# Expert tiles of two 64-row blocks instead of four 32-row blocks, with half of the weights read in place

## The chip, the cores and the metric

One core of one Trainium2 chip. The metric is the device time in microseconds (us) of one execution, the median of several runs. The hardware profiler recorded one further execution; all durations come from it.

## The reference

A transformer block in fp32: layer norm and attention over 2 x 1024 tokens of 256 features, then a mixture of experts. Each of 2048 tokens goes to 4 of 60 experts (8192 choices) and through one shared expert. Cut to the part that the change touches:

```
logits = x @ gate_w.T                          # 2048 x 60
weights, sel = top_k(softmax(logits), 4)
for each expert e:                             # w13_e 352 x 256, w2_e 256 x 176
    gu = x @ w13_e.T
    h  = silu(gu[:, :176]) * gu[:, 176:]
    y += cw[:, e] * (h @ w2_e.T)
out = x + shared(x) + y
```

## The kernel before

The kernel runs attention first, then the shared expert (a hand-written order, `after`, of gate-up, down and routing steps), and last the expert loop over tiles.

**Tiles and blocks.** A tile is 128 rows, cut into `PER` = 4 blocks of `BLK` = 32 rows. A block holds choices of one expert only; an expert with n choices has ceil(n/32) blocks. How many blocks there are is known only on the device, so the loop has a fixed count that suffices for every routing: `NTILE` = ceil((8192/32 + 59)/4) = 79. The tiles that hold choices come first; the rest are padding, computed all the same and scattered to rows that nobody reads. `cnt_i[.., 3, e]` says how many tiles are needed up to expert e.

**Weights.** SP loads the experts in order into a ring of 8 slots (`load_expert`, `refill`): expert e goes out when the last tile of expert e - 8 is done (`tiles_done`). It announces expert e - 2 in `weights_arrived` after the load of e has gone out. A tile's word in `packed` holds the ring slot of each of its blocks and its last expert. VectorE copies each block's gate and up weights (704 elements on 128 partitions) from the ring to `placed13` (`place_gate_up`). ScalarE copies 3 of 4 blocks' down weights (all 4 in each fourth tile), and VectorE the rest, to `placed2`.

**One tile.** PE turns the rows (`turn_rows`, p_xs), multiplies by gate and up (`gate_up`, p_gu: for each of two halves of the features, a matmul for each block, on its own columns of the array), turns h (`turn_h`, p_hT) and multiplies by down (`down`, p_y). VectorE takes the turned rows out (`evacuate`, xsT) and multiplies (hh). ScalarE makes silu (hg), takes hT out (`turn`) and weighs the result into one of `NYS` = 8 buffers (`weigh`, ys). GpSimd scatters ys to `expert_out`; the buffer is free again when the scatter that used it 8 tiles before has landed. In PE's order, iteration i holds turn_rows(i+2), turn_h(i-2), gate_up(i) and down(i-3); the others keep the same order.

**Rows.** GpSimd gathers each tile's 128 rows with one indirect DMA into `xs_low` and `xs_top`, 48 places together. 48 gathers go out before the loop, most of them 4 after each gate-up of the shared expert; the other 31 take places that become free, and are spread over tiles 0 to 62.

**The end.** SP waits until the last tile that holds choices has been scattered, then loads the results in 24 pieces (`fin`). VectorE adds them up, in program order behind all `NTILE` tiles, and SP stores them.

Of the kernel before, what the change touches and what calls it, by code (L numbers as in the profile page):

```python
# [5 lines left out]
def attention_moe_block(nc, x_in, wq_in, wk_in, wv_in, wo_in, gate_in, w13_in, w2_in,  # L6
# [9 lines left out]
    P = 128  # L16
# [25 lines left out]
    PER = 4  # L42
# [11 lines left out]
    N13, N2 = 3, 4  # L54
# [27 lines left out]
    with ctx:  # L82
# [38 lines left out]
        gather_i = keep("gather_i", [P, NTILE], i32)  # L121
# [124 lines left out]
        NXS = min(NTILE, LOW // ROW) // LG * LG  # L246
        xs_low = moe("xs_low", [P, NXS, ROW])
        sb(sm, "low_rest", [P, LOW - used_moe[0]]) if LOW > used_moe[0] else None
        used_moe[0] = 0
        placed2 = moe("placed2", [P, N2, PER, 2 * C])  # L250
# [3 lines left out]

        moe("slot0_kept", [P, PROBS + SLOT_Q - used_moe[0]])
        placed13 = moe("placed13", [P, N13, PER, W13])
        picks = moe("picks", [P, 2, LG, TOPK])
        cw = moe("cw", [P, NTILE])
        ys = moe("ys", [P, NYS, C])
        xsT = moe("xsT", [P, 2, C])  # L260
        MID = PROBS + 3 * SLOT_Q + KV
# [3 lines left out]
        xsT2 = sb(sm, "xsT2", [P, C])  # L265

        NXT = 8
        xs_top = sb(sm, "xs_top", [P, NXT, ROW])
        sm.close()
        xsT = [xsT[:, 0, :], xsT[:, 1, :], xsT2[:, :]]  # L270
# [4 lines left out]
        LAST_TOP = FULL + 2 * LG  # L275
        AGAIN = LAST_TOP - NXS - NXT

        def xs_at(i):

            if i < NXS + NXT:  # L280
                return i, None
            if i < LAST_TOP:
                return i - NXS - NXT, i - NXS - NXT
            return NXS + i - LAST_TOP, NXS + i - LAST_TOP

        def xs_rows(i, n=1):
            at = xs_at(i)[0]
            return xs_low[:, at:at + n, :] if at < NXS else xs_top[:, at - NXS:at - NXS + n, :]

        assert NXS + NXT <= FULL and NTILE - LAST_TOP <= NXT and not (NXS % LG or NXT % LG or LAST_TOP % LG)  # L290

        PART = TQ * C
        LAST_SLOT = (E - 1) % RING
        assert (FULL - NXS - NXT) * ROW >= TOPK * PART and LOW - AGAIN * ROW >= TOPK * PART
        assert LAST_SLOT * WE >= 3 * PART + PART // 2 and (RING - 1 - LAST_SLOT) * WE >= TOPK * PART + PART // 2
        sf = ExitStack()
        fin2 = sb(sf, "fin2", [P, TOPK, TQ, C])
        sb(sf, "rows_kept", [P, AGAIN * ROW - TOPK * PART])  # L300
        fin1 = sb(sf, "fin1", [P, TOPK, TQ, C])
        sb(sf, "mid_kept", [P, LOW - AGAIN * ROW - TOPK * PART + MID])
        fin3 = sb(sf, "fin3", [P, TOPK - 1, TQ, C])
        fin3_a = sb(sf, "fin3_a", [P, 2, C])
        sb(sf, "last_expert_kept", [P, (LAST_SLOT + 1) * WE - 3 * PART - PART // 2])
        fin0 = sb(sf, "fin0", [P, TOPK, TQ, C])
        fin3_b = sb(sf, "fin3_b", [P, 2, C])
# [130 lines left out]
        w2_placed_low = sem("w2_placed_low")  # L438
        w2_placed_high = sem("w2_placed_high")
        xs_loaded = [sem(f"xs_loaded{q}") for q in range((NXS + NXT) // LG)]  # L440
# [97 lines left out]
        def results(k, from_, to):  # L538
            c = from_ // TQ
            from_, to = from_ - c * TQ, to - c * TQ  # L540
            if c == NCH - 1 and k == TOPK - 1:
                return fin3_a[:, from_:to, :] if to <= 2 else fin3_b[:, from_ - 2:to - 2, :]
            return (fin0, fin1, fin2, fin3)[c][:, k, from_:to, :]

        def group_loaded(q):

            n = min(LG, NTILE - q * LG)
            return xs_loaded[xs_at(q * LG)[0] // LG], 16 * (n if q * LG < NXS + NXT else LG + n)

        def downs_on_act(i):  # L550

            return PER if i % 4 == 3 else PER - 1

        def downs_on_dve(i):
            return sum(PER - downs_on_act(n) for n in range(i + 1))
# [125 lines left out]
        def _(pool):  # L681
# [193 lines left out]
            gathered = NXS + NXT - 4 * (NCH * NFS - THIRD)  # L875
            for i in range(gathered):
                gather(i)
            for n in range(THIRD, NCH * NFS):
                pool.wait_ge(sgu_in_psum, n + 1)
                for _ in range(4):  # L880
                    gather(gathered)
                    gathered += 1

# [9 lines left out]
            for n in range(rest):  # L893
                due.setdefault(max(n * (NTILE - 14) // rest, xs_at(gathered + n)[1] + 3), []).append(gathered + n)
# [8 lines left out]
        def _(act):  # L903
# [96 lines left out]
            def place_down(i, from_, to, tile=None):  # L1000
                if from_ == 0:
                    tile = act.value_load(packed[0:1, i:i + 1])
                    if i >= N2:
                        act.wait_ge(tiles_done, i - N2 + 1)
                    wait_apart(act, weights_arrived, tile >> (3 * PER))
                for h in range(from_, to):
                    last = copy(placed2[0:FH, i % N2, h, :], ring[0:FH, W13:][:, bass.ds(ring_at(tile, h), 2 * C)])
                if to == downs_on_act(i):
                    last.then_inc(w2_placed_low, 1)
                return tile  # L1010
# [17 lines left out]
            for i in range(NTILE + 3):  # L1028
                if 2 <= i < NTILE + 2:
                    turn(i - 2)  # L1030
                if i < NTILE:
                    tile = place_down(i, 0, 2)
# [4 lines left out]
                    place_down(i, 2, downs_on_act(i), tile)  # L1037
# [4 lines left out]
        def _(dve):  # L1042
# [368 lines left out]
            def blocks():  # L1411
# [16 lines left out]
                for h in range(PER):  # L1428
# [6 lines left out]
                count(v.scalar_tensor_tensor(out=two[:, 0:2], in0=slots[:, 1:4:2], scalar=float(RING),  # L1435
                                             in1=slots[:, 0:4:2], op0=ALU.mult, op1=ALU.add))
                count(v.scalar_tensor_tensor(out=four[:, 0:1], in0=two[:, 1:2], scalar=float(RING ** 2),
                                             in1=two[:, 0:1], op0=ALU.mult, op1=ALU.add))
                count(v.scalar_tensor_tensor(out=four[:, 1:2], in0=whose[:, 3:4], scalar=float(RING ** PER),
                                             in1=four[:, 0:1], op0=ALU.mult, op1=ALU.add))  # L1440
# [62 lines left out]
            def place_gate_up(i, from_, to, tile=None):  # L1503
                if from_ == 0:
                    tile = dve.value_load(packed[0:1, i:i + 1])
                    if i >= N13:
                        dve.wait_ge(gu_in_psum, i - N13 + 1)
                    wait_apart(dve, weights_arrived, tile >> (3 * PER))
                for h in range(from_, to):
                    last = v.tensor_copy(placed13[:, i % N13, h, :], ring[:, bass.ds(ring_at(tile, h), W13)])  # L1510
                if to == PER:
                    last.then_inc(w13_placed, 1)
                return tile

            def place_down(i, tile):
                if i >= N2:
                    dve.wait_ge(tiles_done, i - N2 + 1)
                for h in range(downs_on_act(i), PER):
                    v.tensor_copy(placed2[0:FH, i % N2, h, :], ring[0:FH, W13:][:, bass.ds(ring_at(tile, h), 2 * C)])\
                        .then_inc(w2_placed_high, 1)  # L1520
# [7 lines left out]
            words = {}  # L1528
            for kind, c, f in after:
# [24 lines left out]
                elif kind == "down" and (c < NCH - 1 or f):  # L1554
                    for q in (2 * f, 2 * f + 1):
                        add_shared(c, q)
                elif kind == "down":

                    h_low_part(NCH * NFS - 1)
                    words[0] = place_gate_up(0, 0, PER)  # L1560
                    add_shared(c, 0)
                    words[1] = place_gate_up(1, 0, PER)
                    add_shared(c, 1)
                elif kind not in ("soft", "late"):
                    on_bench(kind, c, f)
# [15 lines left out]
            for i in range(NTILE):  # L1581
# [5 lines left out]
                if i + 2 < NTILE:  # L1587
                    words[i + 2] = place_gate_up(i + 2, 0, PER - 1)
# [5 lines left out]
                if i + 2 < NTILE:  # L1594
                    place_gate_up(i + 2, PER - 1, PER, words[i + 2])
                place_down(i, words.pop(i))
# [13 lines left out]
        def _(pe):  # L1610
# [246 lines left out]

            def gate_up(i):
# [90 lines left out]
```

## Time and profile before

| what | value |
|---|---|
| median of 3 runs | 739.28 us (736.56 to 745.55) |
| span of the profiled execution | 799.1 us |
| TensorE clock granted, mean | 0.927 |
| busy: PE, DVE, ACT, POOL | 689.1, 482.4, 507.8, 379.1 us |
| attention, shared expert and routing | 0 to 517 us |
| expert loop | 517 to 776 us |
| adding up and storing | to 799 us |

The span reaches from the first to the last instruction. The profiled execution has no other time of its own on record, and its span is 59.8 us longer than the median of the runs. PE is TensorE (PEld its weight loads), DVE VectorE, ACT ScalarE, POOL GpSimd, SP the engine that issues most DMAs.

### The profile page before, as it was taken

The numbers are of one execution on the slowest core, as the hardware profiler recorded it, in microseconds if no ns is written. First come the engines' busy times: TensorE is split into PE (matmuls) and PEld (weight loads), VectorE is DVE, ScalarE is ACT, GpSimd is POOL, SyncE is SP. The second block draws the span as 40 slices with busy tenths as digits, with TensorE's granted clock in tenths as the row PEclk, the third lists the DMA queues.
The fourth block names the chain that finished last, engine by engine and source line by source line (L and its number), as shares of the span: only waits on it lengthen the run. The fifth ranks groups of instructions, "written<-read, shape, count | busy, mean of one in ns | idle before, by whom it ended". The sixth has DMA issues, their size and how long they took to land.

```text
span 799.1 us, 17758 instructions
## 1 busy us (share of the span) xinstructions
PE 689.1 (86%) x5591; PEld 349.4 (44%) x5591; DVE 482.4 (60%) x1335; ACT 507.8 (64%) x865; POOL 379.1 (47%) x376
## 2 busy tenths in 40 slices
PE   3788999999999999987979667699899988989970
PEld 2433333434333443366758455444344433434430
DVE  5784533564524545256864213399587957968957
ACT  2586888878689888922222102099587968868950
POOL 2173242234322293343034727158754875886850
PEclk9799999999899999999989878699889999998985
DMA  5000000000040000092011313146656666765188
GB/s 173 0 2 1 1 1 1 1 1 28 28 135 1 28 28 27 29 215 56 27 3 54 107 32 103 27 128 201 196 162 215 198 186 208 211 193 150 55 276 310
DMA packets 42941, 75.88 MB, mean 95 GB/s; under 512 B 7864, under 2 KB 23676, under 8 KB 42852
## 3 DMA queue, kind: packets, MB, share of 16 engines
q1 hardware_dynamic: 33476, 53.81, 22.1%
q0 software_dynamic: 9376, 20.97, 9.3%
q8 instruction: 45, 0.74, 0.4%
q14 instruction: 44, 0.36, 0.2%
HBM read 58.07 MB, written 16.67 MB: 94 GB/s over the span
## 4 chain that ended last, share of the span: by engine, by line
PE 65%; DVE 13%; issue 7%; another core or an unknown queue 5%; DMA 3%; SPq 3%; ACT 2%; POOL 1%; DVEq 1%; ACTq 0%; POOLq 0%
PE p_o L1694 15%; PE p_gu L1865 10%; PE p_s L1682 10%; PE p_y L1886 6%; PE p_xs L1855 3%; PE bench L1629 2%; SPq L670 2%; PE p_hT L1875 2%; PE p_d L1796 2%; PE bench L1616 1%; PE p_d L1797 1%; PE p_d L1798 1%; PE bench L1730 1%; PE bench L1708 1%
## 5 line engine op out<-in xcount | busy, mean ns | idle before, releaser
L969 ACT ACTIVATE probs<-p_s 128x1024 f32<-128x1024 f32 x256 | 243.8, 1039 | 52.1 <-PE p_s L1682 50.1
L886 POOL DMA_INDIRECT expert_out<-ys,goes_to x79 | 134.7, 1704 | 81.0 <-ACT ys L905 62.8
L905 ACT ACTIVATE placed<-ring 88x512 f32 x256 | 150.4, 626 | 31.3 <-PE p_d L1798 23.4
L1510 DVE COPY placed<-ring 128x704 f32 x316 | 151.7, 520 | 29.1 <-SPq L651 12.2
L1694 PE MATMUL p_o<-probs,vext 128*32 128x512 f32 x1024 | 138.2, 614 | 0.2 <-DVE enr L1176 0.2
L1865 PE MATMUL p_gu<-placed,xsT 128*32 128x352 f32 x1264 | 122.4, 473 | 5.7 <-issue 5.4
L866 POOL DMA_INDIRECT xs_low<-x_rows,choice_i x64 | 76.3, 1191 | 53.0 <-DVE choice_i L1479 17.5
L1682 PE MATMUL p_s<-qst,kst 64*128 64x512 f32 x512 | 95.8, 451 | 3.1 <-DVE kst L1359 1.6
L812 POOL DMA_INDIRECT members<-place,slot x48 | 47.8, 995 | 104.0 <-PE p_o L1694 85.6
L1886 PE MATMUL p_y<-placed,hT 88*32 88x256 f32 x1264 | 91.4, 392 | 2.2 <-ACT hT L905 1.2
L1682 PEld LDWEIGHTS p_s<-qst,kst 64*128 64x128 f32 x512 | 39.4, 185 | 82.3 <-ACT probs L969 62.7
L1886 PEld LDWEIGHTS p_y<-placed,hT 88*32 88x32 f32 x1264 | 45.4, 113 | 44.5 <-issue 30.3
L1865 PEld LDWEIGHTS p_gu<-placed,xsT 128*32 128x32 f32 x1264 | 35.5, 110 | 55.6 <-issue 53.4
L726 POOL TENSOR_TENSOR rc_t<-raw,cos 128x320 f32<-128x320 f32 (+2 forms) x16 | 11.3, 709 | 95.3 <-DVE qst L1369 61.9
L905 ACT ACTIVATE shT_h<-sh 128x512 fp32r<-128x512 f32 (+1 forms) x24 | 15.1, 631 | 64.5 <-PE p_d L1798 28.0
L1796 PE MATMUL p_d<-sdown_h,shT_h 128*128 128x256 f32 (+1 forms) x96 | 32.4, 338 | 18.7 <-DVE xres L1500 13.5
L905 ACT ACTIVATE ys<-p_y,cw 128x256 f32<-128x256 f32 x79 | 36.8, 466 | 15.9 <-remote 10.0
L989 ACT ACTIVATE sg<-p_g 128x512 f32<-128x512 f32 (+1 forms) x20 | 11.9, 594 | 46.9 <-PE p_u L1788 30.5
L1694 PEld LDWEIGHTS p_o<-probs,vext 128*32 128x32 f32 x1024 | 20.4, 108 | 39.5 <-issue 20.9
L1875 PE MATMUL p_hT<-ident,hh 128*88 128x128 f32 x158 | 31.2, 277 | 7.3 <-issue 4.9
L1036 ACT ACTIVATE hg<-p_gu 128x176 f32<-128x176 f32 x79 | 24.1, 305 | 20.2 <-remote 17.6
L1526 DVE COPY xsT<-p_xs 128x256 f32<-128x256 f32 x79 | 32.5, 412 | 5.4 <-remote 4.2
(262 smaller groups left out, 1117.7 us busy)
## 6 DMA issues: line engine op xcount, KB each, us to landing
ring<-in_w_dram SPq DMA_DIRECT2D x60, 352.0 KB
ring<-in_w_dram SPq DMA_DIRECT2D x60, 176.0 KB
fin<-expert_out SPq DMA_DIRECT2D x12, 512.0 KB, 8.6
x_rows<-rows SPq DMA_DIRECT2D x4, 520.0 KB, 3.6
x2T_kept<-xt SPq DMA_DIRECT2D x3, 512.0 KB, 3.6
x2r<-x2T_kept SPq DMA_DIRECT2D x3, 512.0 KB, 6.1
out_dram<-xres SPq DMA_DIRECT2D x3, 512.0 KB, 5.2
sup<-in_sup_dram SPq DMA_DIRECT2D x2, 704.0 KB
```

What stands on the lines that cost most here:

```text
L812: pool.indirect_dma_start(members, bass.IndirectOffsetOnAxis(ap=slot[:, n:n + 1], axis=0), place[:, n:n + 1], None).then_inc(scattered, 16)
L866: pool.indirect_dma_start(xs_rows(i)[:, 0, :], None, x2_rows, bass.IndirectOffsetOnAxis(ap=choice_i[:, 1, i:i + 1], axis=0))\
L886: pool.indirect_dma_start(expert_out, bass.IndirectOffsetOnAxis(ap=goes_to[:, i:i + 1], axis=0), ys[:, i % NYS, :], None).then_inc(y_out[i ...
L905: return nc.scalar.activation(o, i_, ACT.Copy, **kw)
L969: nc.scalar.activation(probs[:, j % NPB, :], p_s[j % NSB][:, :], ACT.Exp, scale=SCALE)\
L1510: last = v.tensor_copy(placed13[:, i % N13, h, :], ring[:, bass.ds(ring_at(tile, h), W13)])
L1682: last = mm(p_s[j % NSB][:, h * QC:(h + 1) * QC], kst[b][rows_, rr // 2, at], qst[rows_, c % 3, pair, :], start=True, stop=True)
L1694: last = mm(p_o[32 * g_:32 * g_ + 32, :], vext[c // 2][:, kb, rr // 2 + KP * h, :], probs[:, (2 * u + half) % NPB, h * QC:(h + 1) * QC], s ...
L1796: mm(p_d[q % 2][:, 0:C], h_high_, high, start=(f == 0), stop=False)
L1865: last = mm(p_gu[i % 2][h * BLK:(h + 1) * BLK, 0:F2], xsT[i % 3][:, k * P + h * BLK:k * P + (h + 1) * BLK], placed13[:, i % N13, h, k * F2 ...
L1875: last = tr(p_hT[i % 2][0:FH, k * P:(k + 1) * P], hh[:, i % 3, k * FH:(k + 1) * FH], ident[:, :])
L1886: last = mm(p_y[i % 2][h * BLK:(h + 1) * BLK, 0:C], hT[0:FH, i % 3, k * P + h * BLK:k * P + (h + 1) * BLK], placed2[0:FH, i % N2, h, k * C ...
```

## The change

Blocks have 64 rows and a tile has two of them, so a fixed count of 94 tiles. PE reads the first block's weights from the ring at an address from a register; only the second block's are copied: gate and up by VectorE, down by ScalarE. PE loads each tile's word for it. Every tile has its own place for its rows, so that no gather waits for a place; 26 gathers go out before the loop and 68 in it. `placed2` has 5 buffers instead of 4. The memory is laid out anew, and the results are loaded to one stretch.

```diff
-    PER = 4
+    PER = 2
     BLK = P // PER
     NTILE = -(-(TOK * TOPK // BLK + E - 1) // PER)
-    N13, N2 = 3, 4
+    N13, N2 = 3, 5
...
             def gather(i):
-                had = xs_at(i)[1]
-                if had is not None:
-                    pool.wait_ge(xsT_in_psum, had + 1)
-                    pool.wait_ge(picks_made, had // LG + 1)
-                elif i == NXS:
-                    pool.wait_ge(sgu_in_psum, (NCH - 1) * NFS)
+                if i == EARLY:
+                    pool.wait_ge(sdown_in_psum, NT)
...
-            gathered = NXS + NXT - 4 * (NCH * NFS - THIRD)
+            gathered = 4
...
-                for _ in range(4):
+                for _ in range(2):
...
-                due.setdefault(max(n * (NTILE - 14) // rest, xs_at(gathered + n)[1] + 3), []).append(gathered + n)
+                due.setdefault(n * (NTILE - 14) // rest, []).append(gathered + n)
...
+            def place_down(i):
+                tile = act.value_load(packed[0:1, i:i + 1])
+                if i >= N2:
+                    act.wait_ge(tiles_done, i - N2 + 1)
+                act.wait_ge(w13_placed, i + 1)
+                copy(placed2[0:FH, i % N2, :], ring[0:FH, W13:][:, bass.ds(ring_at(tile, 1), 2 * C)])\
+                    .then_inc(w2_placed, 1)
...
+            def place_gate_up(i):
+                tile = dve.value_load(packed[0:1, i:i + 1])
+                if i >= N13:
+                    dve.wait_ge(gu_in_psum, i - N13 + 1)
+                wait_apart(dve, weights_arrived, tile >> (3 * PER))
+                v.tensor_copy(placed13[:, i % N13, :], ring[:, bass.ds(ring_at(tile, 1), W13)]).then_inc(w13_placed, 1)
...
                 for k in range(KC):
                     for h in range(PER):
+                        weights = (placed13[:, i % N13, k * F2:(k + 1) * F2] if h else
+                                   ring[:, bass.ds(ring_at(words[i], 0) + k * F2, F2)])
                         last = mm(p_gu[i % 2][h * BLK:(h + 1) * BLK, 0:F2],
                                   xsT[i % 3][:, k * P + h * BLK:k * P + (h + 1) * BLK],
-                                  placed13[:, i % N13, h, k * F2:(k + 1) * F2], start=(k == 0), stop=(k == KC - 1))
+                                  weights, start=(k == 0), stop=(k == KC - 1))
...
+                if i + 1 < NTILE:
+                    words[i + 1] = pe.value_load(packed[0:1, i + 1:i + 2])
```

`down` changes as `gate_up` does. ScalarE's `place_down(i)` stands after its silu of tile i, VectorE's `place_gate_up` two tiles ahead, and PE's load of the next word between `gate_up(i)` and `down(i - 3)`.

## Rows read from the trace of the kernel before

**Rows 1.** The page's groups: line, engine, tiles, count | busy us, mean ns | idle.
```profile
L1510 DVE COPY placed<-ring 128x704 f32 x316 | 151.7, 520 | 29.1 <-SPq L651 12.2
L905 ACT ACTIVATE placed<-ring 88x512 f32 x256 | 150.4, 626 | 31.3 <-PE p_d L1798 23.4
L1865 PE MATMUL p_gu<-placed,xsT 128*32 128x352 f32 x1264 | 122.4, 473 | 5.7 <-issue 5.4
L1886 PE MATMUL p_y<-placed,hT 88*32 88x256 f32 x1264 | 91.4, 392 | 2.2 <-ACT hT L905 1.2
```

**Rows 2.** The timeline of PE in the expert loop: start us, length us.
```profile
545.19 1.39 PE L1865 MATMUL p_gu<-placed,xsT 128*32 128x352 f32 x16
546.40 1.05 PE L1886 MATMUL p_y<-placed,hT 88*32 88x256 f32 x16
547.38 0.44 PE L1855 MATMUL p_xs<-ident,xs_low 128*128 128x128 f32 x2
547.66 0.38 PE L1875 MATMUL p_hT<-ident,hh 128*88 128x128 f32 x2
547.97 1.39 PE L1865 MATMUL p_gu<-placed,xsT 128*32 128x352 f32 x16
...
564.61 1.39 PE L1865 MATMUL p_gu<-placed,xsT 128*32 128x352 f32 x16
```

**Rows 3.** The same timeline for VectorE.
```profile
547.09 1.38 DVE L1510 COPY placed<-ring 128x704 f32 x3
...
548.40 0.33 DVE L1592 TENSOR_TENSOR hh<-hg,p_gu 128x176 f32<-128x176 f32 x1
```

**Rows 4.** The timeline of PE at the loop's first tile and at tile 70.
```profile
517.33 1.39 PE L1865 MATMUL p_gu<-placed,xsT 128*32 128x352 f32 x16
...
743.83 1.39 PE L1865 MATMUL p_gu<-placed,xsT 128*32 128x352 f32 x16
```

**Rows 5.** The timeline of SP and VectorE at the end.
```profile
763.04 19.51 SPq L670 DMA_DIRECT2D fin<-expert_out  x15
...
770.25 0.42 DVE L1519 COPY placed<-ring 88x512 f32 x1
773.68 1.23 DVE L1602 TENSOR_TENSOR fin<-fin 128x1024 f32<-128x1024 f32 x1 [3.01 <-issue]
...
796.50 0.43 DVE L1607 TENSOR_TENSOR xres<-xres,fin 128x256 f32<-128x256 f32 x1
```

**Rows 6.** The stretch after the loop: busy us (x) of each engine.
```profile
771.00:799.00 28.00, 3.64 (x32) 1.61 (x32) 20.07 (x24) 1.69 (x5) 4.38 (x4) 0.51 0.95 329
```

**Rows 7.** GpSimd's groups, first in the loop, then ahead of it (425 to 505).
```profile
L886 POOL DMA_INDIRECT expert_out<-ys,goes_to x71 | 126.1, 1777 | 74.0 <-ACT ys L905 57.0 <-issue 14.9 <-PE p_xs L1855 1.9
L866 POOL DMA_INDIRECT xs_low<-x_rows,choice_i x24 | 37.6, 1567 | 7.3 <-issue 6.1 <-PE p_gu L1865 0.6 <-remote 0.6
L866 POOL DMA_INDIRECT xs_low<-x_rows,choice_i x40: 940/946/1166, 425.5 to 491.4; - x40
```

**Rows 8.** The timeline of GpSimd from its first scatter.
```profile
526.77 1.71 POOL L886 DMA_INDIRECT expert_out<-ys,goes_to  x1 [23.93 <-ACT ys L905]
...
560.07 1.44 POOL L866 DMA_INDIRECT xs_low<-x_rows,choice_i  x1 [0.30 <-issue]
```

**Rows 9.** The timeline of PE in two stretches where it slows down.
```profile
451.26 0.37 PE L1796 MATMUL p_d<-sdown_h,shT_h 128*128 128x256 f32 x1 [0.36 <-issue]
...
574.24 5.07 PE L1865 MATMUL p_gu<-placed,xsT 128*32 128x352 f32 x13 [0.30 <-issue]
```

**Rows 10.** Stretches before the loop: PE, PEld, DVE, ACT, POOL busy (x), clock, DMA.
```profile
448.00:468.00 20.00, 6.31 (x23) 3.86 (x22) 1.81 (x4) 0.60 (x1) 11.35 (x12) 0.65 0.33 87
495.00:507.00 12.00, 1.44 (x4) 1.07 (x5) 1.60 (x4) 0.00 (x0) 6.01 (x7) 0.50 0.30 79
```

**Rows 11.** Loads of the tile's word: ns min/median/max.
```profile
L1505 DVEq TENSOR_LOAD <-packed x79: 300/304/616, 492.9 to 761.7; - x79
L1002 ACTq TENSOR_LOAD <-packed x79: 273/278/787, 515.5 to 767.0; - x79
```

More of the change, by code:

```diff
@@ L264, in attention_moe_block @@
         ring = sb(sm, "ring", [P, RING * WE])
-        xsT2 = sb(sm, "xsT2", [P, C])
-        NXT = 8
-        xs_top = sb(sm, "xs_top", [P, NXT, ROW])
+        NTHIRD = NTILE - NFIRST - NSECOND
+        xs_third = sb(sm, "xs_third", [P, NTHIRD, ROW])
         sm.close()
-        xsT = [xsT[:, 0, :], xsT[:, 1, :], xsT2[:, :]]
+        xsT = [xsT[:, n, :] for n in range(3)]
         FULL = REAL // P
[L275 to L284, printed above, removed]
-        def xs_rows(i, n=1):
[L287 to L297, printed above, removed]
-        sf = ExitStack()
[L299 to L307, printed above, removed]
+        def xs_rows(i, n=1):
+            if i < NFIRST:
+                return xs_first[:, i:i + n, :]
+            if i < NFIRST + NSECOND:
+                return xs_second[:, i - NFIRST:i - NFIRST + n, :]
+            return xs_third[:, i - NFIRST - NSECOND:i - NFIRST - NSECOND + n, :]
+        assert NCH * TOPK * TQ * C <= FULL * ROW and FULL <= NFIRST
+        sf = ExitStack()
+        fin = [sb(sf, f"fin{c}", [P, TOPK, TQ, C]) for c in range(NCH)]
         sf.close()
@@ L539, in results @@
             c = from_ // TQ
[L540 to L543, printed above, removed]
+            return fin[c][:, k, from_ - c * TQ:to - c * TQ, :]
         def group_loaded(q):
             n = min(LG, NTILE - q * LG)
[L548 to L555, printed above, removed]
+            return xs_loaded[q % (NGRP // 2)], 16 * (n if q < NGRP // 2 else LG + n)
         def ring_at(tile, h):
@@ L998, in _ @@
             h_high_part(NCH * NFS - 1)
[L1000 to L1010, printed above, removed]
+            def place_down(i):
[5 more added lines that the diff above has]
+                    .then_inc(w2_placed, 1)
             def turn(i):
@@ L1434, in blocks @@
                 count(v.tensor_copy(slots, slot_i[:, :]))
[L1435 to L1437 removed]
+                count(v.scalar_tensor_tensor(out=two[:, 0:1], in0=slots[:, 1:2], scalar=float(RING),
+                                             in1=slots[:, 0:1], op0=ALU.mult, op1=ALU.add))
+                count(v.scalar_tensor_tensor(out=four[:, 1:2], in0=whose[:, 1:2], scalar=float(RING ** PER),
                                              in1=two[:, 0:1], op0=ALU.mult, op1=ALU.add))
[L1439 to L1440 removed]
                 v.tensor_scalar(eid_b[:, :], four[:, 1:2].to_broadcast([P, P]), float(RING ** PER), None, ALU.add)\
@@ L1883, in down @@
                     pe.wait_ge(y_ready, i - 1)
+                tile = words.pop(i)
                 for k in range(2):
                     for h in range(PER):
+                        weights = (placed2[0:FH, i % N2, k * C:(k + 1) * C] if h else
+                                   ring[0:FH, W13:][:, bass.ds(ring_at(tile, 0) + k * C, C)])
                         last = mm(p_y[i % 2][h * BLK:(h + 1) * BLK, 0:C],
                                   hT[0:FH, i % 3, k * P + h * BLK:k * P + (h + 1) * BLK],
-                                  placed2[0:FH, i % N2, h, k * C:(k + 1) * C], start=(k == 0), stop=(k == 1))
+                                  weights, start=(k == 0), stop=(k == 1))
                 last.then_inc(tiles_done, 1)
+            words[0] = pe.value_load(packed[0:1, 0:1])
             turn_rows(0)
```

72 lines of the change are left out of this document (25 added, 47 removed).

## The prediction

> **What bounds the kernel now.** I read the page's groups first, then the timeline of each engine inside the expert loop, then the end of the kernel.
>
> The groups show where the weights' copies lie: VectorE makes 316 copies of 520 ns for gate and up, ScalarE 256 copies of 626 ns for down, and PE spends 122.4 and 91.4 us on the two products [rows 1]. That looks like a loop that its copies hold up. The timeline says otherwise. Where the loop runs smoothly, PE's groups follow one another without a break: gate-up at 545.19, down at 546.40, turned rows at 547.38, turned h at 547.66, the next gate-up at 547.97 [rows 2]. Seven tiles take 564.61 - 545.19 = 19.42 us, so a tile takes 2.77 us, and all of it is PE's. VectorE is nearly as full but not the last: its copies start 0.43 us apart (three in 1.38 us, with ends that overlap) [rows 3], so 4.25 of them hold it for 1.83 us, and the rest of its tile (hh, xsT, picks) for some 0.7 us.
>
> The loop as a whole is slower. From the first gate-up to that of tile 70 it is 743.83 - 517.33 = 226.5 us [rows 4]. At 2.77 us 70 tiles are 194.2; the first three are 2.6 us shorter together, since no down product stands in them yet; so 34.9 us are excess. The reader is to see two candidates for it. PE itself slows down in places: 13 matmuls that wait for nothing spread over 5.07 us [rows 9]. And GpSimd's DMAs take 1.8 us (scatters) and 1.6 us (gathers) in the loop, but 0.97 us ahead of it [rows 7].
>
> The end has a limit of its own. SP starts to load the results at 763.04, 19.2 us after the gate-up of tile 70; VectorE has finished the padding tiles at 770.67 and waits for the loads until 773.68 [rows 4, 5]. It then adds for 20.07 us with waits between [rows 6], and the last store lands at 799.1.
>
> **How many tiles.** Counted from the reference's own inputs, the 60 experts get 84 to 200 choices. In blocks of 32 these are 284 blocks, 71 tiles; in blocks of 64 they are 154, 77 tiles. The trace agrees with the first: the loads of results begin behind tile 70. The fixed counts are 79 and 94, so padding grows from 8 tiles to 17.
>
> **Part 1, PE's time for a tile.** A matmul still streams 352 or 256 columns over the same two halves; half as many blocks stand side by side, each twice as wide. Now 16 matmuls of 473 ns fill only 1.21 us, so four run at once [rows 1, 2]. Two at once with half the count fill the same 1.21 us. I take 2.77 us again. Below: nothing becomes shorter, since no stream does. Above: if two wide blocks did not overlap, gate-up and down would take 2.2 us more; the overlap of four in the rows speaks against that. The Trainium skill, "TensorEngine Tiling (Array Packing)", Available Configurations and Theoretical Speedup, gives four tiles at 128x32 and two at 128x64, so the gain is 4x for 32 columns and 2x for 64. By that a 64-row block costs twice a 32-row block, as I have it, and the change earns PE nothing: it pays for more rows.
>
> **Part 2, registers on PE.** Each tile adds one load of the word and four addresses. Such a load takes 0.30 us on VectorE and 0.27 on ScalarE [rows 11]. The word of tile i + 1 is loaded behind gate_up(i), whose 1.2 us of matmuls run meanwhile; in front of it is nothing that waits, behind it are down(i - 3), and through it ScalarE's weighing and SP's refills. Between 0 and 0.30 us a tile, 0 to 28 us; I take 0, since the cover is four times as long. It would go if PE had to finish its queue before such a load.
>
> **Part 3, VectorE and ScalarE.** VectorE loses 3 of 4 copies and the quarter one (1.83 us to 0.43 a tile), ScalarE 1.75 of 2.75. Neither is the last engine, so by itself this is worth nothing. VectorE's word load stays. ScalarE's copy now waits for `w13_placed` behind the silu of the same tile; VectorE made that two tiles before, so the wait costs nothing, and behind it stand only weigh and turn. The ring: an expert takes 1.28 tiles instead of 1.18, so 8 slots last longer, and SP's refills come sooner than needed.
>
> **Part 4, GpSimd.** This is where the copies count. In the smooth stretch 13 DMAs go out between 526.77 and 560.07, one in 2.56 us [rows 8], against 0.97 + 0.30 us ahead of the loop [rows 7]. A tile needs one scatter and 31/65 of a gather, 1.48 DMAs or 3.8 us: more than 2.77. GpSimd falls behind by 1 us a tile until the 8 buffers ys are full, after some 15 tiles; then ScalarE's weighing waits for it. What it gets is the time between VectorE's copies: 2.77 - 1.83 = 0.94 us a tile for 1.08 DMAs, 0.87 us each. 1.48 DMAs need 1.29 us, so the pace is 1.83 + 1.29 = 3.12 us while gathers last, 50 tiles: 50 x 0.35 = 17 us. The Trainium skill, "SBUF — State Buffer", SBUF: two separate sides, names the cause: a DMA from GpSimd's queue needs descriptors written through ports that an fp32 SBUF-to-SBUF copy of VectorE holds. By that rule the rows' 0.97 against 1.6 to 1.8 us is no load of the DMA engines, and the change removes it.
>
> After the change a tile needs 1 + 68/80 = 1.85 DMAs: 1.85 x 1.27 = 2.35 us, plus one copy of 0.43, 2.78. That is on a par with PE and no more; a little above it costs nothing until 8 buffers are used up.
>
> How much of the 34.9 us does a timed run have? From above: 17 us, the sum just made. From below: the profiled span is 59.8 us longer than the median. In 448 to 468 and 495 to 507 PE is busy for 6.3 of 20 and 1.4 of 12 us while its matmuls wait for nothing, with the clock at 0.65 and 0.50 of full [rows 9, 10], so 24 us, and some 5 at half clock behind them, look like the recording's own. That leaves 31 of the 59.8 for the loop's 34.9, and 4 us in timed runs. I take the middle, 11 us, and let all of it go.
>
> **Part 5, the end.** Padding now ends last. After tile 76, 17 more tiles run in 47 us; the loads of results take some 24 of them. VectorE adds only behind tile 93: its hh ends 548.73 - 545.19 = 3.54 us after that tile's gate-up starts [rows 2, 3], the sums take 20.07 us without waits, and 2.2 us remain to the last store: 25.8 us after the gate-up of tile 93. Before, the end came 799.1 - 743.83 = 55.3 us after that of tile 70. A price from rows; between them lies 4 us if the loads still hold up the first sum.
>
> **Ahead of the loop.** 22 gathers fewer there, two reads of the blocks' members fewer: GpSimd only, nobody waits for them. Nothing.
>
> **The sum**, made against the profiled execution: 23 tiles more between the two gate-ups, 23 x 2.77 = +63.8; the end 25.8 - 55.3 = -29.5; together +34.3; less the 11 us of lag: +23.3. The difference is carried over to the median of the runs: 739.3 + 23.3 = 762.6, so 763 us, 3.2% slower.
>
> **The rivals.**
> - *The excess is real.* All or most of the 34.9 us is in timed runs, because of GpSimd, and goes. Then +34.3 - 34.9: 739 to 750 us, no change. For: 3.12 us a tile nearly explains it. Against: the 59.8 us. 0.27.
> - *Faster: the slow stretches of PE are real too, and come from bursts of gathers.* 48 gathers ahead of the loop fall to 26, and 24 us go as well: 739.3 - 0.6 - 24 = 715 us. It decides if these stretches are missing in the profile after. Against: they are just what the timed runs lack. 0.07.
> - *No lag at all in timed runs.* PE sets 2.77 us in both: 774 us. 0.25.
> - *The registers stop PE*, at its upper bound: 763 + 28 = 791 us. 0.10.
> - *The change does not do what it says*: if the last engine were VectorE or ScalarE, a tile would become shorter. Rows 2 leave no room for it.
>
> **How the numbers follow.** My forecast has 0.31, the rivals the rest. About 2% either way (724.5 to 754.1 us) is what a measurement of this kernel can tell from no change. Faster: 0.07. Within: 0.27. Slower: 0.31 + 0.25 + 0.10 = 0.66. The range from 738 to 786 us takes in the first and third rival, and leaves out the faster one and most of the last.
>
> **What would show it.** In the profile after: p_gu x752 with gate-up again 2.77 us apart (above that, parts 1 or 2 are wrong); placed copies x94 on each engine; GpSimd's DMAs near 1.1 us in the loop; loads of results 17 tiles before the loop's end, and VectorE's first sum straight behind its last hh. I would be wrong if timed runs before had the whole excess, or if PE's period changed.

## The result, and the profile after

| | before | after |
|---|---|---|
| median | 742.04 us (736.56 to 745.55, 4 runs) | 758.75 us (756.74 to 762.03, 4 runs) |
| ratio after/before | | 1.022, 95% interval 1.016 to 1.029 |
| profiled execution | span 799.1 us | span 756.8 us, own time 758.59 us |

The change made the kernel 16.7 us slower, 2.2%: clear of no change, though the interval does not tell whether it is more or less than 2%. But the two profiles can't simply be subtracted: the one of before was 60 us longer than its timed runs, and I had put part of this down to the recording. The experiments show what it was. They ran on four chips (all kernels of one section below on the same one). On the first the kernel before takes 741.5 us, on the other three 803.0, 802.4 and 798.5. The comparison above is from a chip of the first kind; the profile of before shows the times of the second. I call them quick and slow chips. Each of the four ran the experiments of one section only, at one time, so what differs may belong to the time and not to the chip; no run here separates the two. The partner for the profile after is therefore the second profile of before, from a quick chip (the first experiment).

The profile after, groups: line, engine, tiles, count | busy us, mean ns | idle.
```profile
L850 POOL DMA_INDIRECT expert_out<-ys,goes_to x94 | 96.6, 1028 | 79.4 <-ACT ys L869 74.4 <-issue 5.0
...
L1807 PE MATMUL p_gu<-ring,xsT 128*64 x376 | 131.4, 472 | 0.0
L1807 PE MATMUL p_gu<-placed,xsT 128*64 128x352 f32 x376 | 131.4, 472 | 0.0
...
L1465 DVE COPY placed<-ring 128x704 f32 x94 | 49.7, 529 | 39.3 <-SPq L618 21.3
...
L869 ACT ACTIVATE placed<-ring 88x512 f32 x94 | 59.4, 631 | 28.3 <-issue 26.0
```
Against [rows 1] a matmul is as long as before (472 and 473 ns), there are 752 instead of 1264, and only two stand side by side. So a tile's gate-up still takes 1.40 us (131.4 / 94; the two groups run over the same time), and there are more tiles. Against [rows 7] a scatter takes 1028 ns instead of 1777, and GpSimd now waits for ys (74.4 us): it is ahead of its work.

The same profile, PE's timeline at the gate-ups of tiles 0 and 93:
```profile
476.52 0.51 PE L1807 MATMUL p_gu<-ring,xsT 128*64 x1
...
732.33 0.51 PE L1807 MATMUL p_gu<-ring,xsT 128*64 x1
```
The same profile, busy time between these two: us, PE, PEld, DVE, ACT, POOL busy (x), clock, DMA.
```profile
476.52:732.33 255.81, 255.81 (x1832) 133.11 (x1831) 122.36 (x325) 144.41 (x366) 156.47 (x157) 1.00 0.74 225
```
PE is busy for all of the 255.81 us at a granted clock of 1.00: nothing holds it up in the loop, and VectorE and ScalarE are busy for about half of the time.

The same profile, SP and VectorE at the end:
```profile
700.13 24.58 SPq L637 DMA_DIRECT2D fin<-expert_out  x24
...
734.13 0.34 DVE L1533 TENSOR_TENSOR hh<-hg,p_gu 128x176 f32<-128x176 f32 x1 [2.21 <-ACT hg L995]
734.38 1.22 DVE L1540 TENSOR_TENSOR fin<-fin 128x1024 f32<-128x1024 f32 x1
```
The loads of results are all out at 724.7, and the first sum comes straight behind the last hh. Where [rows 5] have VectorE waiting for loads, the padding tiles now set the end.

### The profile page after: what moved, and what is told of

Read it like the earlier page. It is cut to its first block, busy times and chain, and to the rows that moved or that the text cites. A ratio compares the mean times of both kernels' runs of the same rounds, so it can differ in the third digit from the quotient of the medians.

```text
span 756.8 us, 15005 instructions
## 1 busy us (share of the span) xinstructions
PE 697.6 (92%) x4627; PEld 365.0 (48%) x4627; DVE 392.5 (52%) x1082; ACT 447.8 (59%) x748; POOL 333.4 (44%) x404
## 4 chain that ended last, share of the span: by engine, by line
PE 84%; DVE 13%; ACT 1%; issue 1%; DMA 1%; DVEq 0%; ACTq 0%
PE p_gu L1807 17%; PE p_o L1632 16%; PE p_s L1620 10%; PE p_y L1830 10%; PE p_xs L1793 5%; PE p_hT L1817 3%; PE bench L1567 2%; PE p_d L1734 2%; PE bench L1554 2%; PE p_d L1736 1%; PE p_d L1735 1%; PE bench L1668 1%; PE bench L1646 1%; PE bench L1684 1%; PE p_g L1724 1%; PE p_g L1725 1%
## 5 line engine op out<-in xcount | busy, mean ns | idle before, releaser
L850 POOL DMA_INDIRECT expert_out<-ys,goes_to x94 | 96.6, 1028 | 79.4 <-ACT ys L869 74.4
L1807 PE MATMUL p_gu<-ring,xsT 128*64 x376 | 131.4, 472 | 0.0
L1807 PE MATMUL p_gu<-placed,xsT 128*64 128x352 f32 x376 | 131.4, 472 | 0.0
L829 POOL DMA_INDIRECT xs_first<-x_rows,choice_i x80 | 77.9, 974 | 69.1 <-issue 19.8
L1830 PE MATMUL p_y<-ring,hT 88*64 x376 | 96.6, 379 | 0.0
L1830 PE MATMUL p_y<-placed,hT 88*64 88x256 f32 x376 | 96.6, 379 | 0.0
L869 ACT ACTIVATE placed<-ring 88x512 f32 x94 | 59.4, 631 | 28.3 <-issue 26.0
L1830 PEld LDWEIGHTS p_y<-ring,hT 88*64 88x64 f32 x376 | 51.1, 136 | 42.2 <-issue 28.1
L1465 DVE COPY placed<-ring 128x704 f32 x94 | 49.7, 529 | 39.3 <-SPq L618 21.3
L1807 PEld LDWEIGHTS p_gu<-ring,xsT 128*64 128x64 f32 x376 | 43.7, 136 | 46.0 <-issue 46.0
L1830 PEld LDWEIGHTS p_y<-placed,hT 88*64 88x64 f32 x376 | 51.0, 136 | 0.0
```

Source lines behind the costliest of these rows:

```text
L829: pool.indirect_dma_start(xs_rows(i)[:, 0, :], None, x2_rows, bass.IndirectOffsetOnAxis(ap=choice_i[:, 1, i:i + 1], axis=0))\
L850: pool.indirect_dma_start(expert_out, bass.IndirectOffsetOnAxis(ap=goes_to[:, i:i + 1], axis=0), ys[:, i % NYS, :], None).then_inc(y_out[i ...
L869: return nc.scalar.activation(o, i_, ACT.Copy, **kw)
L1465: v.tensor_copy(placed13[:, i % N13, :], ring[:, bass.ds(ring_at(tile, 1), W13)]).then_inc(w13_placed, 1)
L1807: last = mm(p_gu[i % 2][h * BLK:(h + 1) * BLK, 0:F2], xsT[i % 3][:, k * P + h * BLK:k * P + (h + 1) * BLK], weights, start=(k == 0), stop= ...
L1830: last = mm(p_y[i % 2][h * BLK:(h + 1) * BLK, 0:C], hT[0:FH, i % 3, k * P + h * BLK:k * P + (h + 1) * BLK], weights, start=(k == 0), stop= ...
```

## Experiments on a quick chip (before: 741.5 us)

All four kernels ran beside 13 runs of the kernel before (737.21 to 748.02 us).

**The kernel before again.** 

> The kernel before once more (with one bound more on the word that VectorE and ScalarE load), to get a second profile of it. My theory: the stretches in which PE slowed down belonged to that one execution; here they are missing, the span is near 740 us, and from the first gate-up to that of tile 70 it takes 196 to 209 us (191.6 at 2.77 us a tile, and 4 to 17 us of lag that GpSimd's DMAs cause). Rival: the excess of 35 us is real; then it takes 226 us again. Rival: no lag, 192 us.

Its edit, on both word loads, also in all kernels below (in those made from the kernel after, on VectorE's alone):
```diff
-                tile = dve.value_load(packed[0:1, i:i + 1])
+                tile = dve.value_load(packed[0:1, i:i + 1], min_val=..., max_val=...)
```
Measured: 740.08 us (737.85 to 746.8), ratio 1.001 (0.997 to 1.005), span of the profile 736.9. PE's timeline at the gate-ups of tiles 0 and 70:
```profile
478.24 1.39 PE L1865 MATMUL p_gu<-placed,xsT 128*32 128x352 f32 x16
...
674.50 1.39 PE L1865 MATMUL p_gu<-placed,xsT 128*32 128x352 f32 x16
```
The loop begins 39 us earlier than in [rows 4], and its 70 tiles take 196.26 us instead of 226.5. So the stalls of [rows 9, 10] are missing, and of the excess of 34.9 us only 4.7 are left. GpSimd lags all the same. The group of scatters in this profile:
```profile
L886 POOL DMA_INDIRECT expert_out<-ys,goes_to x79 | 128.1, 1622 | 24.1 <-issue 20.4 <-ACT ys L905 2.4 <-PE p_xs L1855 0.9
```
The timelines of ScalarE (tile 70's ys), GpSimd (its scatter) and SP:
```profile
690.40 0.50 ACT L905 ACTIVATE ys<-p_y,cw 128x256 f32<-128x256 f32 x1
...
698.68 1.14 POOL L886 DMA_INDIRECT expert_out<-ys,goes_to  x1 [0.30 <-ACT ys L905]
...
702.03 18.20 SPq L670 DMA_DIRECT2D fin<-expert_out  x15
```
The scatter of tile 70 starts 8.3 us behind its ys (3.6 us in the first profile, where stalls of PE had let GpSimd catch up). And the ys itself comes late, 15.9 us after the gate-up for 10.8 in the first profile, since ScalarE had to wait for a buffer:
```profile
679.81 0.47 ACT L905 ACTIVATE ys<-p_y,cw 128x256 f32<-128x256 f32 x1 [3.92 <-DMA expert_out<-ys,goes_to]
```
So the lag comes due at the end: the loads of results can't start before 702.03, and the end is 736.9 - 674.5 = 62.4 us behind tile 70's gate-up (55.3 in the first profile). This gives the account of the change on a quick chip, from span to span:

| | before | after | difference | forecast |
|---|---|---|---|---|
| first gate-up | 478.24 | 476.52 | -1.7 | 0 |
| to that of the last tile that sets the end (70, 93) | 196.26 | 255.81 | +59.6 | +63.8 - 11 |
| from there to the end | 62.4 | 24.5 | -37.9 | -29.5 |
| sum | 736.9 | 756.8 | +19.9 | +23.3 |

**No registers on PE.** 

> The kernel after, with PE reading both blocks' weights from the copies of the second block at constant addresses; PE loads no words. Left out: the first block's own weights. My theory: the word load and the addresses lie beside matmuls and cost nothing, so the time is that of the kernel after, 757 to 761 us. Rival: they stop PE by up to 0.30 us a tile; then the 94 tiles become up to 28 us shorter, 731 us, and the gate-ups stand closer than 2.79 us.


```diff
-                        weights = (placed13[:, i % N13, k * F2:(k + 1) * F2] if h else
-                                   ring[:, bass.ds(ring_at(words[i], 0) + k * F2, F2)])
+                        weights = placed13[:, i % N13, k * F2:(k + 1) * F2]
...
-                if i + 1 < NTILE:
-                    words[i + 1] = pe.value_load(packed[0:1, i + 1:i + 2])
```
(`down` likewise.) Measured: 759.25 us (758.73 to 765.0), ratio 1.024 (1.016 to 1.032). PE's timeline:
```profile
562.92 1.40 PE L1805 MATMUL p_gu<-placed,xsT 128*64 128x352 f32 x8
...
565.71 1.40 PE L1805 MATMUL p_gu<-placed,xsT 128*64 128x352 f32 x8
...
568.49 1.40 PE L1805 MATMUL p_gu<-placed,xsT 128*64 128x352 f32 x8
```
2.79 us a tile with and without registers, and from the gate-up of tile 0 to that of tile 93 it is 255.78 us for 255.81: word loads and addresses are free here. The rival falls.

**No padding tiles.** 

> The kernel after with 77 tiles, those that hold choices for these inputs, and no padding tile. My theory: the 17 padding tiles (47 us) then go, but the loads of results, which they covered, end last: the end comes some 55 us after the gate-up of tile 76 as it did after that of tile 70 before, so 685.4 + 55 = 741 us of span, 16 us less than the kernel after. Rival: the loads end earlier than that and all 47 us go, 712 us. Rival: the end does not depend on the padding, no change.


```diff
-    NTILE = -(-(TOK * TOPK // BLK + E - 1) // PER)
+    NTILE = 77
...
-        NTHIRD = NTILE - NFIRST - NSECOND
+        NTHIRD = LG
```
(The second edit keeps the room for the last tiles' rows as large as one group.) Measured: 730.33 us (728.68 to 732.78), ratio 0.986 (0.978 to 0.994), 28 us less than the kernel after. Tile 76's gate-up on PE, SP, and VectorE's first sum:
```profile
684.13 0.51 PE L1807 MATMUL p_gu<-ring,xsT 128*64 x1
...
694.00 21.49 SPq L637 DMA_DIRECT2D fin<-expert_out  x24
...
702.51 1.23 DVE L1540 TENSOR_TENSOR fin<-fin 128x1024 f32<-128x1024 f32 x1 [16.25 <-DMA fin<-expert_out]
```
Tile 76's gate-up in the kernel after:
```profile
685.44 0.51 PE L1807 MATMUL p_gu<-ring,xsT 128*64 x1
```
As I thought, the loads then end last, but they cost less: 727.7 - 684.1 = 43.6 us behind tile 76, not 55. The 55.3 us of before held 8 padding tiles and GpSimd's lag. Tile 76's down product no longer stands behind three padding tiles, so the loads start 9.9 us after its gate-up (14.7 in the kernel after). The 17 padding tiles take 732.33 - 685.44 = 46.9 us, and the end behind the last gate-up is 43.6 - 24.5 = 19.1 us shorter with them, so they cost 28 us, more than the whole change loses. This kernel holds for these inputs only, not for every routing.

**Busy VectorE, with waits.** 

> The kernel after with four more fp32 copies of 512 elements on VectorE in each tile (some 1.3 us), to a buffer that nobody reads. My theory: these copies block GpSimd's DMAs, as the copies of the kernel before did: a scatter and a gather take 1.6 to 1.8 us instead of 0.97 to 1.2; 1.85 of them a tile no longer fit into 2.79 us, ScalarE's weighing waits for buffers, and the time grows by 15 to 50 us although VectorE itself has room. Rival: the DMAs of before were slow for the weights' and rows' traffic; then they stay at 1.0 to 1.2 us and the time stays at 759 us.


```diff
+                if i >= 2:
+                    for n in range(4):
+                        if i > 2 or n:
+                            dve.wait_ge(junk_made, 4 * (i - 2) + n)
+                        v.tensor_copy(junk[:, :], xres[:, 2 * n:2 * n + 2, :].rearrange("p t c -> p (t c)"))\
+                            .then_inc(junk_made, 1)
```
Measured: 801.84 us (798.69 to 804.45), ratio 1.081 (1.072 to 1.090). The size is about as expected, the cause is not. VectorE's timeline:
```profile
599.71 0.53 DVE L1467 COPY placed<-ring 128x704 f32 x1 [0.20 <-issue]
600.16 1.80 DVE L1472 COPY junk<-xres 128x512 f32<-128x512 f32 x4
601.88 0.33 DVE L1541 TENSOR_TENSOR hh<-hg,p_gu 128x176 f32<-128x176 f32 x1
602.12 0.42 DVE L1479 COPY xsT<-p_xs 128x256 f32<-128x256 f32 x1
602.89 0.53 DVE L1467 COPY placed<-ring 128x704 f32 x1 [0.35 <-issue]
```
The group of scatters:
```profile
L852 POOL DMA_INDIRECT expert_out<-ys,goes_to x94 | 105.6, 1123 | 106.0 <-ACT ys L871 103.0
```
VectorE's own round is now 602.89 - 599.71 = 3.18 us, above PE's 2.79, and in it VectorE waits for no other engine; GpSimd still waits for ys. This run says nothing for the blocking of DMAs; these copies, with a wait before each, lengthen a scatter from 1028 ns to 1123.

## Experiments on a slow chip (before: 803.0 us)

**VectorE's copies alone.** 

> The kernel before, with VectorE's copies of gate and up cut to 8 of 704 elements behind the third tile; all else stays, the gathers and their places too. Left out: most of the gate and up weights that PE should read. My theory: VectorE's long copies are what makes GpSimd's DMAs slow in the loop; without them scatters and gathers take 1.0 to 1.1 us, scatters follow ys by 0.3 us instead of up to 20, and the time falls by some 10 to 12 us (4.7 us in the loop and some 7 us by which the loads of results start earlier), to 728 to 731 us. Rival: something else slows them (ScalarE's copies, the load of the queues, the places of rows that must come free); then the scatters still lag by some 15 us and the time stays within 3 us of 740.


```diff
+                wide = W13 if i < N13 else 8
-                    last = v.tensor_copy(placed13[:, i % N13, h, :], ring[:, bass.ds(ring_at(tile, h), W13)])
+                    last = v.tensor_copy(placed13[:, i % N13, h, 0:wide], ring[:, bass.ds(ring_at(tile, h), wide)])
```
Measured: 791.66 us (790.92 to 794.51) beside 803.0, ratio 0.986 (0.980 to 0.992): -11.3 us, the 10 to 12 that I had expected, though beside another time. GpSimd's group, here and in the first profile of before:
```profile
L886 POOL DMA_INDIRECT expert_out<-ys,goes_to x79 | 77.4, 980 | 150.6 <-ACT ys L905 143.9 <-issue 6.7
...
L886 POOL DMA_INDIRECT expert_out<-ys,goes_to x79 | 134.7, 1704 | 81.0 <-ACT ys L905 62.8 <-issue 16.1 <-PE p_xs L1855 1.9
```
With the long copies gone, and nothing else changed, a scatter falls from 1704 ns to 980, and GpSimd no longer lags. This is the shown part of the theory: in this kernel GpSimd's DMAs are slow only with VectorE's long copies. The Trainium skill, "SBUF — State Buffer", SBUF: two separate sides, says that such a copy keeps GpSimd from writing the descriptors of its DMAs. The trace agrees as to the effect; it shows nothing of the descriptors.

**Part of the copies back.** 

> The kernel after with 77 tiles and, on VectorE, three more copies of 704 elements a tile that follow one another without a wait between them, as in the kernel before (their source is the copy of the tile before, nobody reads them). The run with four copies of 512 elements had a wait before each and was slower because VectorE itself became the last engine, while GpSimd's DMAs stayed at 1.0 to 1.1 us. By my theory, that copies in one piece block GpSimd, the DMAs take 1.6 us or more, scatters fall behind, and the time is 10 to 40 us above that of 77 tiles without them (730 us). Rival: the port is no matter; the DMAs stay at 1.0 to 1.1 us, and with 2.4 us of VectorE's work in 2.79 the time stays within 3 us of 730.


```diff
+                if i > 2:
+                    dve.wait_ge(junk_made, i - 2)
+                if i >= 2:
+                    for n in range(3):
+                        last = v.tensor_copy(junk[:, n, :], placed13[:, (i - 1) % N13, :])
+                    last.then_inc(junk_made, 1)
```
(704 columns each, on top of the kernel with 77 tiles.) Measured: 753.05 us (750.08 to 755.37), ratio to this chip's before 0.938 (0.932 to 0.945). Its partner (730 us) ran on a quick chip, so the time decides nothing. GpSimd's group:
```profile
L852 POOL DMA_INDIRECT expert_out<-ys,goes_to x77 | 90.3, 1173 | 68.5 <-ACT ys L871 56.0 <-issue 12.6
```
Four copies in a row give 1173 ns, not the 1600 that I expected; the kernel before has 1704 with 4.25. So without the long copies the slowness goes, but adding copies does not bring it back. What else takes part in the kernel before was not tried: there ScalarE copies 3.25 blocks a tile and here 1, and the added copies read another buffer. The ratio of 0.938 was the first sign of something else: its first gate-up comes at 475.7 us, where the kernel before, on such a chip, has 517.33 [rows 4].

**The first block from the ring.** 

> The kernel before, four blocks of 32 rows, with PE reading each tile's first block of weights from the ring; VectorE copies 3 blocks of gate and up instead of 4, ScalarE 2 or 3 of down. My theory: VectorE has 0.45 us a tile more in which GpSimd's DMAs run free; the lag falls and most of the 12 us that it costs come back: 728 to 735 us, faster than both kernels. Rival: the lag does not come from VectorE's copies: 740 us.


```diff
+                        weights = (placed13[:, i % N13, h, k * F2:(k + 1) * F2] if h else
+                                   ring[:, bass.ds(ring_at(words[i], 0) + k * F2, F2)])
```
(`down` likewise.) VectorE now makes 3 copies of gate and up a tile and 0.5 of down (4 and 0.25 before), ScalarE 2.5 of down (3.25 before). Measured: 789.72 us (787.93 to 794.3), ratio 0.986 (0.979 to 0.993). The 728 to 735 us were for a quick chip; the gain of 13 us is about the one expected.
```profile
L886 POOL DMA_INDIRECT expert_out<-ys,goes_to x79 | 87.4, 1106 | 132.1 <-ACT ys L905 123.6 <-issue 7.8 <-DVE picks L1573 0.7
```
So one block fewer takes most of the slowness away: 1106 ns with VectorE's 3.5 copies a tile, 1704 with 4.25, 980 with almost none. ScalarE's copies are fewer here too, so the step from 4.25 to 3.5 is not VectorE's alone.

**No padding before.** 

> The kernel before with 71 tiles, no padding tile. My theory: padding costs the kernel before next to nothing, since its 8 tiles end at 703 us while the results' loads start at 702 us and their first lands at 712; what goes is the wait of tile 70's down product for three further tiles, as far as GpSimd's lag does not take its place: 732 to 740 us. Rival: all 8 tiles count, 22 us less, 718 us.


```diff
+    NTILE = 71
```
Measured: 787.22 us (785.36 to 789.8), ratio 0.982 (0.976 to 0.989): -15.8 us, twice what I allowed. From tile 70's gate-up to the end it is 783.6 - 738.1 = 45.5 us instead of 55.3; the tiles up to it are 4.9 us shorter, one execution against another. Padding was not free before either. This splits the loss on a quick chip, as an estimate across two kinds of chip: 28 - 16 = 12 us for more padding, 6 x 2.79 = 17 us for six more tiles that hold choices, less the 12 us that GpSimd's lag had cost (below).

## Experiments on a second slow chip (before: 802.4 us)

**The kernel after, here.** 

> The kernel after once more (with one bound more on the word that VectorE loads). The kernel before has run at 742 us on two occasions and at 803 us on a third, where, as in the first profile of it, PE stalls ahead of the loop. My theory: such stalls are a chip's answer to GpSimd's gathers in bursts, and the kernel after does not make these bursts; so it takes some 759 to 780 us whatever the kernel before takes beside it, and where that takes 803 it is faster by 3 to 5%. Rival: the stalls belong to the chip and hit both kernels; then the ratio stays 1.02 and it takes 815 to 820 us beside 803.

Measured: 792.39 us (789.56 to 797.08, 9 runs), ratio 0.990 (0.987 to 0.994). Here the change is no loss but a gain of 10 us, 1%. I had expected 759 to 780 us, and by the rival 815 to 820: both were wrong. The span is 789.7, PE's timeline at the gate-ups of tiles 0 and 93:
```profile
477.28 0.51 PE L1807 MATMUL p_gu<-ring,xsT 128*64 x1
...
765.23 0.51 PE L1807 MATMUL p_gu<-ring,xsT 128*64 x1
```
The busy time between them:
```profile
477.28:765.23 287.95, 271.25 (x1831) 134.79 (x1830) 116.25 (x325) 139.25 (x366) 156.77 (x157) 0.98 0.65 200
```
Against the first profile of before the loop starts 40.0 us earlier, takes 287.95 - 226.5 = 61.5 us more and the end 24.5 - 55.3 = 30.8 less: -9.4. The loop is 32 us longer than the same loop on the quick chip (255.81). The view of waits, 478 to 765 us, names what the engines waited for (us in total, times, longest):
```profile
ACT hg L995 <- remote: 32.9, 13, 3.9
...
DVE xsT L1471 <- remote: 29.2, 14, 4.7
...
ACT hT L869 <- remote: 16.8, 7, 3.7
...
ACT ys L869 <- remote: 14.0, 8, 2.3
```
"remote" is the profile's name for a wait that no instruction of this core ended. The profile after from the quick chip has no such line.

**Bursts of gathers in the kernel after.** 

> The kernel after with 40 gathers ahead of the loop instead of 26, four behind each gate-up of the shared expert as in the kernel before, and 54 in the loop instead of 68. My theory: where the kernel before takes 803 us, PE stalls ahead of the loop as it does in that kernel, the first gate-up comes at 505 to 517 us instead of 476, and the time grows by 25 to 40 us; where it takes 742 us nothing happens, within 3 us of the kernel after. Rival: bursts are no matter, no change in either case.


```diff
-                for _ in range(2):
+                for _ in range(4 if gathered < EARLY else 0):
```
Measured: 788.63 us (785.4 to 795.55), ratio 0.988 (0.979 to 0.997), so 4 us less than the kernel after (their runs overlap) and not 25 to 40 more. Yet the first half of the theory holds. Its timeline in the shared expert, where the gathers begin to come in a row:
```profile
441.44 0.28 PE L1734 MATMUL p_d<-sdown_h,shT_h 128*128 128x256 f32 x1
...
441.73 0.94 POOL L829 DMA_INDIRECT xs_first<-x_rows,choice_i  x1 [0.30 <-issue]
442.61 0.28 PE L1735 MATMUL p_d<-sdown_l,shT_h 128*128 128x256 f32 x1 [0.89 <-issue]
442.97 0.94 POOL L829 DMA_INDIRECT xs_first<-x_rows,choice_i  x1 [0.30 <-issue]
...
443.33 0.37 PE L1736 MATMUL p_d<-sdown_h,shT_l 128*128 128x256 f32 x1 [0.44 <-issue]
443.35 0.60 ACT L953 ACTIVATE sg<-p_g 128x512 f32<-128x512 f32 x1 [3.69 <-remote]
```
Matmuls that ran 0.12 us apart come 0.7 to 1.2 us apart, ScalarE stands for 3.69 us, and GpSimd goes on with a gather in 0.94 us. The first gate-up comes at 496.32, 19 us later than without bursts. The loop gives it back: 262.8 us between the gate-ups of tiles 0 and 93 instead of 287.95, with 54 gathers in it instead of 68.

**Fewer gathers in the kernel before.** 

> The kernel before with 26 gathers ahead of the loop instead of 48, two behind each gate-up instead of four, and 53 in the loop instead of 31. My theory: where the kernel before takes 803 us, the first gate-up comes at 476 to 480 us instead of 517, and the time falls by 35 to 40 us less what 22 more gathers cost in the loop, where a tile now has 1.8 DMAs of GpSimd beside 1.8 us of VectorE's copies: 3.2 to 3.5 us a tile for 65 tiles would give back 20 to 40 us. So 765 to 800 us there, and 760 to 780 us where the kernel before takes 742. Rival: bursts are no matter, and the time only grows.


```diff
-            gathered = NXS + NXT - 4 * (NCH * NFS - THIRD)
+            gathered = 4
...
-                for _ in range(4):
+                for _ in range(2):
```
(`due`, the list of gathers in the loop, is made to take the tiles that need not wait for a place.) Measured: 787.01 us (784.92 to 792.86), ratio 0.985 (0.977 to 0.993). The loop starts at 479.76, 37 us earlier than in [rows 4], and gives 22 of them back (248.7 us to tile 70 instead of 226.5), as expected.

One stretch of the shared expert shows the effect side by side. Windows of 440 to 460 us: us, PE, PEld, DVE, ACT, POOL busy (x), clock, DMA. Two gathers a step, the kernel after on this slow chip:
```profile
440.00:460.00 20.00, 19.78 (x118) 17.18 (x117) 6.76 (x12) 4.61 (x8) 6.95 (x8) 1.00 0.20 51
```
Two a step, the kernel before with fewer gathers, same chip:
```profile
440.00:460.00 20.00, 19.78 (x117) 17.09 (x116) 7.07 (x12) 4.28 (x7) 6.99 (x8) 1.00 0.20 53
```
Four a step, the kernel after with bursts, same chip:
```profile
440.00:460.00 20.00, 4.97 (x25) 3.47 (x24) 1.94 (x4) 0.60 (x1) 11.50 (x13) 0.66 0.34 89
```
Four a step, the first profile of before:
```profile
440.00:460.00 20.00, 13.37 (x62) 9.38 (x60) 4.09 (x6) 3.05 (x5) 15.12 (x17) 0.85 0.39 103
```
Four a step, the kernel before, quick chip:
```profile
440.00:460.00 20.00, 19.78 (x118) 17.18 (x117) 7.04 (x12) 4.32 (x7) 15.18 (x16) 1.00 0.36 101
```
It takes both: bursts (13 to 17 of GpSimd's instructions in 20 us) and a slow chip. PE then does 25 to 62 matmuls where it did 118; in the same window the three kernels on the first slow chip that kept their bursts have 51, 58 and 59, and the one without (77 tiles) 117.

## The version that beats both (slow chip, before: 798.5 us)

> Two changes to the kernel before that earlier runs point to: PE reads each tile's first of four blocks from the ring, so that VectorE copies 3 blocks a tile, and 26 gathers go out ahead of the loop instead of 48, two behind each gate-up. My theory: GpSimd's DMAs take 1.11 us each as they did with the first change alone, so 1.67 a tile take 2.35 us and fit into 2.77; beside a kernel before at 802 us the first gate-up comes at 477 to 480 us and not at 517, the stalls in the loop stay, and it takes 758 to 775 us; beside one at 742 us the lag of 12 us goes, and it takes 728 to 737 us. Both are faster than before and after. Rival: what the shorter start gives is given back by 22 more gathers in the loop, as with 26 gathers alone (787 us beside 802); then 780 to 790 us, or no change beside 742.

The edits are those of the two sections on the first block from the ring and on fewer gathers, together. Measured: 771.68 us (769.07 to 776.38, 6 runs), ratio 0.968 (0.964 to 0.972). The first gate-up comes at 479.84, and the scatters are quick:
```profile
L886 POOL DMA_INDIRECT expert_out<-ys,goes_to x79 | 87.6, 1108 | 102.0 <-ACT ys L906 91.9 <-issue 7.9 <-DVE picks L1574 1.5
```
On slow chips this kernel saves 27 us on the one before, where the change saved 10. It was not timed on a quick chip; 728 to 737 us there is a forecast, no result.

## The prediction, point by point

- *PE sets a tile, before and after (parts 1 and 3): right.* 2.79 us against 2.77. Eight matmuls of two wide blocks take 1.40 us where sixteen of four narrow ones took 1.39 [rows 2]; the Trainium skill, "TensorEngine Tiling (Array Packing)", Available Configurations, has four tiles at 128x32 and two at 128x64, and the trace agrees. The 0.01 to 0.02 us more (some 1 us in all) is there without registers too, so it comes with some other part of the change; which one was not tried.
- *Registers are free (part 2): right*, by the run without them.
- *GpSimd's lag (part 4): there, but not where I had it.* I took 11 us, all in the loop. On a quick chip it is 4.7 us in the loop and, through the late loads of results, the 62.4 - 55.3 = 7.1 us of the end. That the two make 11.8 is luck: the 11 was the middle of two bounds, and neither counted the end. That VectorE's copies are needed for it is shown, that they are enough is not. My upper bound, 17 us in the loop, came from dividing VectorE's free time among the DMAs; but PE kept 2.77 us from tile 4 (487.14) to tile 30 (559.26) while scatters came 15 to 22 us behind ys, so the model was too hard.
- *The end (part 5): the mechanism right, the size off.* After: 24.5 us for 25.8, because the last hh ends 2.14 us after its gate-up starts; I had read 3.54 from a tile in the middle of the loop. Before: 62.4 for 55.3, since I read it from an execution in which stalls had let GpSimd catch up.
- *"Ahead of the loop: nothing": right on a quick chip (-1.7 us), wrong on a slow one (-40 us).*
- *The slow stretches "look like the recording's own": this step failed.* All 30 timed runs of before on slow chips have the excess (793.2 to 810.9 us), and the three profiles of kernels there that kept its bursts start the loop at 516.5 to 518.6 us. The conclusion, that the runs to be compared lack them, held because these ran on a quick chip, and not for my reason: this was luck. The rival that I gave 0.07, bursts of gathers, is the right mechanism for the stretches ahead of the loop, [rows 10] and the first line of [rows 9]; the second line, at 574 us, is in the loop and is not explained by it. The rival also misses that on such a chip the loop takes most of the gain back. Had the comparison been made on a slow chip, the change would have been 1% faster, some 732 us when carried over to 739.3, outside my range from 738.

The forecast of +23.3 us against +19.9 (spans) or +16.7 (medians) is thus right in its main sum, 64 us of tiles against 30 us of end and some lag. That it is also close is in part luck: the loop came out 6.8 us worse than forecast (59.6 for 52.8) and the end 8.4 us better. What stays open: why PE, ScalarE and VectorE stall on slow chips when GpSimd issues many DMAs. Each starts single instructions late, and no row shows what they wait for. That the stalls in the loop come from gathers rests on two pairs that also differ ahead of it (32 us of them with 68 gathers in the loop, 7 with 54), so it is likely and not shown.

## What to carry to other kernels

A fixed count that suffices for every routing is work: wider blocks doubled the padding tiles, from 8 to 17, and the 17 cost 28 us, more than the 12 us of lag that went with the copies. When the last engine has no gap, look behind it for the engine whose lag comes due only at the end, here GpSimd between VectorE's copies: in the kernel before 980 ns a scatter without them, 1106 with 3.5 a tile, 1622 to 1704 with 4.25 (but 1173 with 4 in the kernel after). And when a profile is much longer than the timed runs, take another one, if possible on another chip, before calling its stalls noise: spreading the gathers was worth 37 us ahead of the loop on slow chips, of which 15 were left in the end (787.0 us beside 802.4).

## What the hardware showed that I had not expected

Four chips ran the same kernel in 741.5 and in 803.0, 802.4 and 798.5 us, at a granted clock of 1.00 in the smooth stretches of both. On the slower ones, 20 us with 13 of GpSimd's instructions left PE with 25 matmuls instead of 118, at a granted clock of 0.66. And four copies of 512 columns with a wait before each cost VectorE 1.80 us a tile and GpSimd little (1123 ns a scatter for 1028).
